# Softmax weights laid out with the heads innermost and combined on TensorE, an earlier first chunk, and a bound on indirect DMAs in flight

## What is computed

```python
gains = softmax(q @ W_qscale.T + scale_gain.T, axis=-1)      # 11 scales for each of 16 heads
for j in range(11):
    for tau, h_coef in enumerate(D4):                        # 4 coefficients
        offset = (1 << j) * tau                              # shift in steps, skipped from 512 on
        qk = sum(q * shift(k, offset), axis=-1)
        out += gains[..., j] * h_coef * qk * shift(v, offset)
out += softplus(bypass) * sum(q * k) * v
x += (out * sigmoid(gate)) @ W_out.T + b_out
x += experts(layernorm(x))                                   # gelu(x @ W1[e] + b1[e]) @ W2[e] + b2[e]
x += layernorm(scan(h = tanh(h @ A.T + x @ B.T)) @ C.T + x)  # 512 steps, in order
x += experts(layernorm(x))
```

## Time and profile before

| | us |
|---|---|
| median of 3 runs (1463.11 to 1469.2) | 1468.77 |
| the profiled execution | 1470.49 |
| its span, first to last instruction | 1468.3 |
| busy: PE, DVE, POOL, ACT | 1169.1, 796.2, 795.5, 653.2 |
| granted TensorE clock, mean share of full speed | 0.852 |

### The profile page before, as it was taken

How to read it: one execution, slowest core, us unless ns; L and a number is a source line. 1 busy time by engine, 2 the same in 40 slices (tenths; PEclk the granted TensorE clock), 3 DMA queues, 4 the chain that set the end, 5 groups by cost and what they waited for, 6 DMA issues and landing times.

```text
span 1468.3 us, 32909 instructions
## 1 busy us (share of the span) xinstructions
PE 1169.1 (80%) x9942; PEld 882.6 (60%) x9942; DVE 796.2 (54%) x1723; ACT 653.2 (44%) x2050; POOL 795.5 (54%) x1274
## 2 busy tenths in 40 slices
PE   3878876787978898899987898867987697995581
PEld 2645444565656675566564666766866576784571
DVE  4877799889875786667777576321123111130011
ACT  2233332555445645556554563543642343452241
POOL 2655457655688558836378948764146414013604
PEclk9998998998989989989999898787986576686786
DMA  4700001221222212111123212233332242343452
GB/s 125 207 1 0 1 1 49 70 66 58 77 64 55 61 33 80 48 49 38 41 68 85 66 48 82 82 96 96 105 93 85 60 121 81 85 118 107 124 136 69
DMA packets 117639, 107.59 MB, mean 73 GB/s; under 512 B 15540, under 2 KB 88541, under 8 KB 117469
## 3 DMA queue, kind: packets, MB, share of 16 engines
q1 hardware_dynamic: 106704, 88.01, 21.1%
q0 software_dynamic: 8192, 16.79, 3.8%
q10 hardware_dynamic: 2573, 0.69, 0.2%
HBM read 76.73 MB, written 28.70 MB: 72 GB/s over the span
## 4 chain that ended last, share of the span: by engine, by line
PE 38%; POOL 22%; DVE 14%; issue 10%; ACT 6%; another core or an unknown queue 6%; ACTq 1%; DMA 1%; SPq 1%; DVEq 1%; POOLq 0%
PE bank L1143 10%; PE bank L1130 9%; POOL acc L792 9%; PE bank L1170 4%; POOL mom L757 4%; POOL back L824 3%; DVE made L1295 3%; DVE term L1324 2%; POOL sorted_x L812 2%; PE bank L1066 2%; PE bank L1034 2%; PE bank L1013 2%; PE bank L1107 1%; PE bank L1123 1%
## 5 line engine op out<-in xcount | busy, mean ns | idle before, releaser
L792 POOL TENSOR_TENSOR acc<-acc,term 128x512 f32<-128x512 f32 x219 | 281.9, 1287 | 61.0 <-DVE term L1324 42.5
L1143 PE MATMUL bank<-w,hT 128*128 x1088 | 216.7, 323 | 27.6 <-ACT hT L968 15.6
L988 ACT ACTIVATE hid<-bank 128x16 f32<-128x16 f32 x512 | 93.6, 183 | 255.5 <-PE bank L1170 207.5
L968 ACT ACTIVATE hT<-bank,b1T 128x128 f32<-128x128 f32 x544 | 166.4, 372 | 84.5 <-PE bank L1130 67.9
L824 POOL DMA_INDIRECT back<-sorted_y,slot_i x128 | 126.9, 992 | 137.4 <-DMA sorted_y<-ysb 51.7
L1170 PEld LDWEIGHTS bank<-hid,abcT 128*32 128x32 f32 x4096 | 88.4, 116 | 187.3 <-ACT hid L988 104.6
L1143 PEld LDWEIGHTS bank<-w,hT 128*128 128x128 f32 x1088 | 173.4, 220 | 45.8 <-issue 40.3
L1324 DVE TENSOR_TENSOR term<-bank,V 128x512 f32<-128x512 f32 x251 | 167.9, 683 | 59.9 <-PE bank L1093 29.1
L1170 PE MATMUL bank<-hid,abcT 128*32 128x16 f32 x4096 | 138.4, 201 | 65.1 <-ACT hid L988 60.0
L1295 DVE SCALAR_TENSOR_TENSOR made<-bank,qkvb,K 128x512 f32<-128x512 f32 x251 | 176.1, 742 | 17.8 <-PE bank L1066 7.6
L1130 PE MATMUL bank<-xTb,w1b 128*128 128x128 f32 x864 | 164.8, 318 | 3.1 <-ACT xTb L956 2.5
(11 more groups left out here) (177 smaller groups left out, 2214.3 us busy)
## 6 DMA issues: line engine op xcount, KB each, us to landing
w1b<-in_W SPq DMA_DIRECT2D x130, 256.0 KB
K<-in_W SPq DMA_DIRECT2D x54, 256.0 KB, 2.7
xsb<-sorted_x SPq DMA_DIRECT2D x184, 64.0 KB
sorted_y<-ysb SPq DMA_DIRECT2D x136, 64.0 KB
X<-in_x SPq DMA_DIRECT2D x64, 64.0 KB
out_x<-X SPq DMA_DIRECT2D x64, 64.0 KB
sorted_x<-K SPq DMA_DIRECT2D x14, 256.0 KB, 3.7
sorted_y<-made SPq DMA_DIRECT2D x48, 64.0 KB
```

The costliest lines, as they stand in the source:

```text
L792: nc.gpsimd.tensor_tensor(acc[:], acc[:] if k > 1 else term[0][:], term[k % NTERM][:], ALU.add).then_inc(S["terms_added"], 1)
L968: last = nc.scalar.activation(tile(hT[u], c), tile(bank[SLOT_BANK[u]], c), ACT.Gelu, bias=b1T[:, ds(bias[n] + c, 1)])
L988: nc.scalar.activation(hid[n % 2][:, cs], bank[6 + n % 2][:, cs], ACT.Tanh).then_inc(S["h_ready"], 1)
L1143: last = nc.tensor.matmul(bank[SLOT_BANK[place(n)]][:, 0:D], tile(hT[place(n)], c), w2[:, ds(second[n] + c * D, D)], start=(c == 0), stop= ...
```

## The change

Three things change in the code.

1. **Weights.** Within a tile the gains lie as (scale, head), with an empty row of 16 in front, so that a window of 128 columns is 8 scales x 16 heads and the window 16 columns earlier is one scale less. `scale` and `wshift` go. `rows` for the offsets 3*2^m stays 4 transposes. For the offsets 2^m it becomes 4 pairs of matmuls, gains times the identity plus one scale less times `ratio` (the identity times D4[2]/D4[1]), and so does the one for offset 256 (from chunk 8 on). The coefficient is applied in `rcopy`. Max and sum over scales now step 16 columns from element to element; a memset of 64 columns is added to each chunk. Product j lies in buffer (j + 2) % 7, so only products 5 and 6 overwrite gains and wait for `rows`.
2. **Start.** W_qkv is one load, six of the loads go to SP behind the first four tiles of x, `scale_gain` is read in one run. DVE takes the statistics of chunk 0 ahead of the derived weights; PE waits for the transposed weights only, and `setup_done` is waited for by the first `logit` and the first `tanh`. Later statistics are held back.
3. **Indirect DMAs.** In scatters from job 4 on and gathers from job 3 on, POOL waits for the indirect DMA three before the next one, on semaphores that are now one for each tile of a chunk.

The costs in `timeline()` for `rows` rise (0.8 to 2.4 and 2.0), so all orders are planned anew. The part of the diff that matters:

```diff
+UNDER_WAY = 3
+LIMIT_SCATTER, LIMIT_GATHER = 4, 3
+GAINS_OVERWRITTEN = (5, 6)
...
+def product_buffer(j):
+    return (j + 2) % NPROD
...
+STATS_AFTER = [[], [], [("shift", 0, 1)], [("product", 0, len(products(0)) - 1)], [("product", 1, len(products(1)) - 1)]]
...
-        for g in (0, 2, 1):
-            if g < 2 or g2:
-                piece("ACT", "scale", i, g, 1.1 if g < 2 else 0.25, USUAL, [("gmul", i, 0)])
-        for k in range(TPC):
-            piece("DVE", "wshift", i, k, 0.46, USUAL, [("scale", i, 0)])
-        if g2:
-            piece("DVE", "wshift", i, TPC, 0.32, USUAL, [("scale", i, 2)])
         for g in (1, 0, 2):
             if g < 2 or g2:
                 free = [("low", before, 2 * g + h) for h in range(len(halves(before, g)))] if i and g < 2 else [] if g < 2 else \
                     [("spread", before, last_term(before, 2)) if i and active(before)[2] else None]
-                piece("PE", "rows", i, g, 0.8, USUAL,
-                      [("scale", i, 1) if g == 1 else ("wshift", i, TPC - 1 if g == 0 else TPC)] + free, bank0=1)
+                piece("PE", "rows", i, g, [2.4, 0.8, 2.0][g], USUAL, [("gmul", i, 0)] + free, bank0=1)
                 piece("ACT", "rcopy", i, g, 0.62, USUAL, [("rows", i, g)], bank0=0)
         for j, s in enumerate(prods):
             free = [("reduce", i, batch_of(i, j - NPROD))] if j >= NPROD else []
-            if j < NPROD:
-                free = [("scale", i, 0), ("scale", i, 1), ("wshift", i, TPC - 1), ("rows", i, 0), ("rows", i, 1)]
-                if g2:
-                    free += [("rows", i, 2)]
+            if j in GAINS_OVERWRITTEN:
...
-        gains, gmax, gsum = made[:, 0:w], made[:, w:w + TPC * H], made[:, w + TPC * H:w + 2 * TPC * H]
-        w8 = made[:, w + 2 * TPC * H:w + 3 * TPC * H]
-        w01 = prod[2:4]
+
+        w = TPC * H * (NS + 1)
+        gains_tile = [made[:, c * H * (NS + 1):(c + 1) * H * (NS + 1)] for c in range(TPC)]
+        all_gains = made[:, 0:w].rearrange("p (c s h) -> p c s h", c=TPC, h=H)
+        gains, no_gains = all_gains[:, :, 1:NS + 1, :], all_gains[:, :, 0, :]
...
+                if c == 0:
+                    for j, n in enumerate(["W_out", "A", "B", "C"]):
+                        sp.dma_start(tile(wload, 4 + j), a[n]).then_inc(S["weights_in"], 16)
+                    sp.dma_start(small[0:NE, 0:D], a["Wg"]).then_inc(S["weights_in"], 16)
+                    sp.dma_start(small[0:32, P:2 * P], a["b1"].rearrange("e (c p) -> (e c) p", p=P)).then_inc(S["weights_in"], 16)
...
+                    if n >= LIMIT_SCATTER and k >= UNDER_WAY:
+                        c, q = divmod(k - UNDER_WAY, TPC)
+                        pool.wait_ge(scattered[n % 2][q], tiles_scattered(n) - 16 * (JOB[n].chunks - c - 1))
...
+                    if n >= LIMIT_GATHER and k >= UNDER_WAY:
+                        c, q = divmod(k - UNDER_WAY, TPC)
+                        c += CHUNKS_BEFORE[n]
+                        pool.wait_ge(back_in[c % 2][q], 16 * (c // 2 + 1))
...
-            act.wait_ge(S["setup_done"], 1)
...
-                elif what == "scale":
-                    act.wait_ge(S["gains_ready"], nth("gmul", n))
-                    if k < 2:
-                        ins = nc.scalar.activation(w01[k].rearrange("p (c m h) -> p c m h", c=TPC, h=H),
-                                                   by_scale[:, :, 0:8, :], ACT.Copy, scale=D4[1] if k == 0 else D4[3])
-                    else:
-                        ins = nc.scalar.activation(w8.rearrange("p (c h) -> p c h", c=TPC), by_scale[:, :, 8, :],
-                                                   ACT.Copy, scale=D4[1])
-                    ins.then_inc(S["scaled"], 1)
...
-            pe.wait_ge(S["setup_done"], 1)
-            pe.wait_ge(S["norm_in"], 16 * 3)
+            pe.wait_ge(S["weights_taken"], 1)
...
+                    if n == 0 and k == 0:
+                        pe.wait_ge(S["setup_done"], 1)
...
-                    if k == 1:
-                        pe.wait_ge(S["scaled"], nth("scale", n, 1))
-                    else:
-                        pe.wait_ge(S["w_shifted"], nth("wshift", n, TPC - 1 if k == 0 else TPC))
+                    pe.wait_ge(S["gains_ready"], nth("gmul", n))
                     for c in range(TPC):
-                        if k < 2:
-                            last = nc.tensor.transpose(tile(bank[0], c), tile(w01[k], c), ident)
+                        own, one_less = (gains_tile[c][:, x:x + (P if k < 2 else H)] for x in ((H, 0) if k < 2 else (9 * H, 8 * H)))
+                        if k == 1:
+                            last = nc.tensor.transpose(tile(bank[0], c), own, ident)
                         else:
-                            last = nc.tensor.transpose(bank[0][0:H, c * P:(c + 1) * P], w8[:, c * H:(c + 1) * H], ident)
+                            dst = bank[0][0:P if k == 0 else H, c * P:(c + 1) * P]
+                            nc.tensor.matmul(dst, own, ident, start=True, stop=False)
+                            last = nc.tensor.matmul(dst, one_less, ratio[:], start=False, stop=True)
...
+            for place_in_order, (what, n, k) in enumerate(ORDER["DVE"]):
+                if place_in_order == 1:
+                    derive_weights()
...
-                elif what == "wshift":
-                    dve.wait_ge(S["gains_ready"], nth("gmul", n))
-                    dve.wait_ge(S["scaled"], nth("scale", n, 0 if k < TPC else 2))
-                    if k < TPC:
-                        dst, src = w0v[:, k, 1:8, :], by_scale[:, k, 0:7, :]
-                    else:
-                        dst, src = w8.rearrange("p (c h) -> p c h", c=TPC), by_scale[:, :, 7, :]
-                    V_.scalar_tensor_tensor(out=dst, in0=src, scalar=D4[2], in1=dst, op0=ALU.mult, op1=ALU.add).then_inc(
-                        S["w_shifted"], 1)
...
-                        dve.wait_ge(S["w_shifted"], nth("wshift", n, TPC if active(n)[2] else TPC - 1))
-                        dve.wait_ge(S["scaled"], max(nth("scale", n, g) for g in range(3 if active(n)[2] else 2)))
-                        if active(n)[2]:
-                            dve.wait_ge(S["bank0_filled"], in_turn("rows", n, 2))
-                    if k == 2:
-                        dve.wait_ge(S["bank0_filled"], max(in_turn("rows", n, 0), in_turn("rows", n, 1)))
+                    if k in GAINS_OVERWRITTEN:
+                        dve.wait_ge(S["bank0_filled"], max(in_turn("rows", n, g) for g in range(3 if active(n)[2] else 2)))
```

165 lines of the change are left out of this document (87 added, 78 removed).

## The result

The changed kernel takes 1490.8 us (median of four runs, 1475.12 to 1493.2) against 1468.99 for the kernel before in the same comparison: ratio 1.0142, interval 1.008 to 1.0204. It is slower, where I had forecast 3% faster; rival 3, at 1487, is the number that came nearest. The profiled execution takes 1490.02 us. Some executions of a kernel come out over 1.5% above its fastest, at a lower granted clock, and the ratios and medians here leave them out.

A forecast was written before the change was run, and what follows sets the result against it. It took a DVE and POOL chain as the bound at first, crowded PE later, and PE alone after the attention. -11 - 4 - 40 - 6 + 18 + 0 = -43 on 1470.5 gave 1427.5, taken as 1426; range 1405 to 1446.

The forecast's parts named there:

- rival 3: Recurrence after the attention: 54 more steps, 43 us of chain, push chunk 10 and all behind it; 1487 us, chance 0.10.
- Start, -11: Kernel start: the first transpose of x comes at 15.3 instead of 26.3 us, gated by ACT; 11 us saved.
- Chunk 0, -4: First attention chunk: products 0 to 4 run during the softmax instead of waiting for combined weights; 4 us saved.
- Chunks 1 to 9, -40: Attention up to 500 us: `wshift` removed and five products moved among the adds save 4.5 us a chunk, 40 in all.
- Product 5's wait, 0: Attention chunks: product 5 now waits for `rows`, which stands two thirds into the adds, so no cost.
- The premise: After 910 us PE leads the chain, so attention gains arrive nearly whole unless PE has more left to do.
- PE's side, +3 a chunk: `rows` on PE: 1.5 us more a chunk, 3.0 from chunk 8; chunks 10 to 15 still net -6 us.
- After the attention, +18: After the attention: 54 more recurrence steps and 4 more slots left over for PE cost 18 us.
- Indirect DMAs, 0: Scatters and gathers: POOL's new wait seldom holds anything, worth 0 us, with bounds +10 and -40.
- immunity from GpSimd's path: Scatter bursts: a Trainium skill page says SP's DMAs never touch GpSimd's descriptor path; by it the bound is worth 0.
- Rival 1: Scatter and gather bursts: the bound on indirect DMAs frees SP, 40 us more saved, 1386 us; chance 0.14.
- rival 4: Sum and max over scales on DVE: 64-byte steps cost 1.5 us a chunk, 24 in all, 1450 us; chance 0.09.

The follow-up runs named there:

- second series: Follow-up runs against the kernel before, including the changed kernel unaltered (1.0058) and the kernel before with the bound on indirect DMAs alone (1.0053).
- a_place: Changed kernel with product j back in buffer j % 7 and orders planned anew, against the kernel before: 1474.53 us, 1.011.
- a_hold: Changed kernel with the queries of chunks 9 to 12 held back in the plan, against the kernel before: 1387.34 us, 1.0173.
- b_work: Kernel before, same orders, with `rows` transposes for offsets 2^m and 256 done twice as full matmuls, against the kernel before: 1.0095.
- a_nopair: Changed kernel, same orders, with one transpose in place of each pair of matmuls in `rows`, against the kernel before: 1.0122.

## Why the prediction was wrong

- **Start, -11: right for the transpose, half of it at the first `resid`.** The transpose came at 14.35, with DVE's copies of the weights ahead of it and not ACT. (The working also has a misread row: of the 6.1 us from the statistics to the transpose the statistics were 0.87 and not 3.5, POOL's moments the most.) Alone in the kernel before the new start moved the first `resid` by 5 us and the last by 7 (76.5 and 919.9 against 81.8 and 927.1, from profiles of different series), and the time by 0.1 to 1.6%.
- **Chunk 0, -4: there, and lost.** Its first term came at 49.0 us, with the start alone at 53.1. At its `resid` 0.8 us of this was left (75.7 and 76.5).
- **Chunks 1 to 9, -40: the step that failed first.** It took the 6.7 us from `gmul` to the first product as DVE's own chain and 681 ns as what each `wshift` would give back. Cut to a column, `wshift` lost 21 of its 49 us, and the last `resid` came 8.4 us earlier (918.7, against 927.1 in a profile of another series), and the whole gained at most 0.5%. Gone entirely, with the new rows in its place, it gave the attention nothing (927.0 against 919.9). A third of the operations, with two thirds of the time, were lengthened beside POOL's adds; at chunks 1 to 3 product 0 had to wait for the adds in any case, by way of the `gate` ahead of it on DVE, and from chunk 10 on `wshift` was not what it waited for. I had named this bound ("if the adds or the shared bank set all, nothing") and judged the place to be of the other sort from one chunk's idle times. What sets product 0 at chunks 4 to 9 the runs leave open.
- **Product 5's wait, 0: wrong.** It cost 30.8 us of idle time, 8.7 of it in chunk 0, though not all of it on the path. "Two thirds into the adds" left out that `rows` waits for `gmul`, which waits its turn on POOL.
- **The premise, "should arrive at the end nearly whole": wrong, and it weighs most.** It came from a chain that PE leads after 910 us. But where the attention got early, expert slots got late, whose rows the recurrence needs: 29.5 us gained and none left (second series), 35 us given up for nothing (a_place), 22 us traded without gain (a_hold). It holds only for time that is added with the order fixed: 38 us more on DVE cost 34 by the medians.
- **PE's side, +3 a chunk: right for the work, too much for the time.** The pairs take 2.05 us where the forecast had 2.2, but the same work without the rest cost 13 us (b_work) of the 36 that 1.5 and 3.0 a chunk make. Its removal gave nothing back (a_nopair) and went with a lower granted clock; which of the two brings the other the runs do not show.
- **After the attention, +18: right in sign, wrong in cause.** The last state came 29 us later. It was not the 54 steps: chunk 10 begins when job 3's rows are there, 38 us late, and a_place, with a hole of 70 us ahead of it, begins it no earlier. Rival 3 forecast a late recurrence and came nearest with its number, 1487, but it had the steps as the cause; that the number fits is luck. What came late are the jobs, 1 and 2 by 55 us and 3 by 38. Why job 3 is as late in a_place, where job 2 is late by 18 us only, stays open.
- **The range.** It was said to rest on -20 and +18 around -40, but the part's own bounds, 0 and -58, are +40 and -18. With these it reaches 1466, and is still 25 us short of what was measured.
- **Indirect DMAs, 0: near.** Alone 0.5% slower, at the edge of what can be told. SP's standstill in the burst speaks neither for nor against immunity from GpSimd's path, as I had it: the trace doesn't name what SP waited for. Rival 1 fell: the unknown waits were 87 us before and 90 after, and the longest stood in the scatters of job 7 as before.
- **Strided reads, rival 4: half right.** The sum went from 876 to 1367 ns, a factor of 1.56, so the stride does cost on DVE; the max over scales stayed (15.6 us in all for 16.7 before). The rule of the page "SBUF — State Buffer" of the Trainium skill, section "Door 1: The DMA port swizzle", agrees with the sum; the max reads PSUM and says nothing on it. What I held against it was misread: the 246 ns are the shortest of the operations of 64 columns, while the shortest of 112 columns took 326 (2.9 ns a column).
- **What I left out: the order.** The planner's new cost alone made the kernel before 1.4 to 2.8% slower. Taken out together with the bound, the rest of the change is level with the kernel before (0.9976), and the start has a share in that: the start alone was 14 us faster in the same series. So the new weights cost about 1%, the plan and the bound about another, the start gives about 1% back. These shares come in part from different series and are no better than half a per cent each. How much of the shown 1.4% is the plan and how much the bound, the runs leave open.

## What to carry to other kernels

Before you count a removed operation as a gain, find what the next instruction on its engine waits for: if that is another engine's queue, the time turns into idle time in front of the same instruction. Where two streams share the fullest engine, a gain in one can be a loss in the other, so show first which of them the end waits for. An experiment that shrinks an operation is a removal only if its recorded time goes too: add it up. And where a planner writes the order, measure the new plan by itself, with the old work: here two numbers in it were worth as much as the change.
